# Spreading biases by TensorE, a root on ScalarE, scores that begin with high halves: one change to a fused layer kernel

## The reference

```python
xn  = (x - mean(x)) / sqrt(var(x) + 1e-5)
# branch 1, per sequence
h   = tanh(xn @ W1.T + b1)                 # 256 -> 256
s   = h @ w2.T + b2                        # one score for each token
e   = exp(s - max(s))
ctx = cumsum(e * xn) / cumsum(e)           # running mean over the tokens
a   = tanh(concat(ctx, xn) @ Wc.T + bc)    # 512 -> 256
# branch 2, integer weights / 127
f   = (silu(xn @ wg.T) * (xn @ wu.T)) @ wd.T   # 256 -> 768 -> 256
out = x + a + f
```

## Time and profile before

| | us |
|---|---|
| median of 3 runs | 412.07 |
| the profiled execution | 412.01 |
| its span, first to last instruction | 410.1 |
| TensorE busy | 391.7 |
| VectorE busy | 300.6 |
| ScalarE busy | 252.3 |
| GpSimd busy | 194.4 |

### The profile page before, as it was taken

The page is one execution under the profiler, slowest core; times in us unless marked ns, Lnnn a source line. Parts: engine busy times, 40 slices in busy tenths (PEclk is TensorE's granted clock), DMA queues, the critical chain, the costliest instruction groups (busy, mean ns, idle before and its releaser), DMA issues.

```text
span 410.1 us, 7885 instructions
## 1 busy us (share of the span) xinstructions
PE 391.7 (96%) x2742; PEld 269.3 (66%) x2742; DVE 300.6 (73%) x636; ACT 252.3 (62%) x465; POOL 194.4 (47%) x256
## 2 busy tenths in 40 slices
PE   7689989999979999899999999999999999999996
PEld 2435746675737578577768676676767677685765
DVE  3897988998896889785874857778668577755351
ACT  1797768888979775684563764536354553536250
POOL 0251342556643999868370512878707365402000
PEclk9898999999999999999999999999999999999999
DMA  6998221334334163647200012332331240101001
GB/s 207 362 349 262 54 52 40 64 57 74 74 81 127 34 131 95 136 91 143 77 28 27 26 53 55 107 98 69 90 77 40 89 105 2 51 14 41 27 26 59
DMA packets 55039, 36.84 MB, mean 90 GB/s; under 512 B 31696, under 2 KB 50384, under 8 KB 54992
## 3 DMA queue, kind: packets, MB, share of 16 engines
q1 hardware_dynamic: 54416, 35.79, 33.3%
q10 hardware_dynamic: 576, 0.46, 0.5%
HBM read 20.45 MB, written 8.45 MB: 70 GB/s over the span
## 4 chain that ended last, share of the span: by engine, by line
PE 62%; DVE 10%; POOL 8%; issue 7%; ACT 6%; DMA 4%; SPq 2%; ACTq 0%; POOLq 0%; DVEq 0%
PE bank L623 31%; PE bank L650 24%; PE bank L670 6%; POOL xt L1103 3%; POOL ex L1095 2%; DVE stats L857 2%; DMA xt<-xt 2%; SPq L1135 2%; ACT xnat L760 2%; DMA xres<-in_x 2%; POOL wide L1113 2%; DVE bank L995 2%; ACT bank L783 1%; POOL ex L1100 1%; ACT sg L789 1%
## 5 line engine op out<-in xcount | busy, mean ns | idle before, releaser
L650 PE MATMUL bank<-xt,narrow 128*128 128x512 f16 x768 | 178.2, 380 | 2.4 <-DVE sm L932 2.2
L650 PEld LDWEIGHTS bank<-xt,narrow 128*128 128x128 f16 x768 | 75.1, 98 | 79.7 <-DVE sm L932 2.7
L623 PE MATMUL bank<-narrow,xt 128*128 128x256 f16 x768 | 94.4, 276 | 5.5 <-DMA xt<-xt 2.4
L623 PE MATMUL bank<-narrow,wide 128*128 128x256 f16 x792 | 96.3, 273 | 0.0
L623 PEld LDWEIGHTS bank<-narrow,xt 128*128 128x128 f16 x768 | 75.5, 99 | 25.2 <-issue 3.5
L623 PEld LDWEIGHTS bank<-narrow,wide 128*128 128x128 f16 x792 | 77.5, 98 | 9.4
L1113 POOL TENSOR_TENSOR wide<-ex,wide 128x512 f16<-128x512 f32 x32 | 40.0, 1267 | 83.8 <-ACT wide L810 83.8
L789 ACT ACTIVATE sg<-bank 128x512 f32<-128x512 f32 x96 | 56.8, 593 | 37.2 <-PE bank L650 37.0
L995 DVE SCALAR_TENSOR_TENSOR bank<-bank,sg 128x512 f32<-128x512 f32 x96 | 65.6, 693 | 15.9 <-PE bank L650 13.5
L1000 DVE TENSOR_TENSOR wide<-bank,wide 128x512 f16<-128x512 f32 x90 | 60.4, 680 | 20.3 <-ACT wide L796 18.7
L796 ACT ACTIVATE wide<-bank 128x512 f16<-128x512 f32 x90 | 53.4, 595 | 34.2 <-DVE bank L995 33.7
(11 more groups left out here) (84 smaller groups left out, 237.4 us busy)
## 6 DMA issues: line engine op xcount, KB each, us to landing
rows<-scratch SPq DMA_DIRECT2D x16, 512.0 KB, 5.4
out_y<-xres SPq DMA_DIRECT2D x32, 256.0 KB, 2.2
xres<-in_x SPq DMA_DIRECT2D x15, 512.0 KB, 8.8
xt<-xt SPq DMA_TRANSPOSE x56, 2.5
wide<-in_wg SPq DMA_DIRECT2D x1, 768.0 KB, 9.2
wide<-in_wu SPq DMA_DIRECT2D x1, 768.0 KB, 9.8
wide<-in_wd SPq DMA_DIRECT2D x1, 768.0 KB, 11.9
xres<-in_x SPq DMA_DIRECT2D x2, 256.0 KB, 5.8
```

Source lines behind the costliest of these rows:

```text
L623: return pe.matmul(dst, lhs, rhs, start=False, stop=stop, skip_group_check=True)
L650: mm = pe.matmul(b[:, :], pg.up(which, k, j), pg.xn(sx, k, tok), start=n == 0, stop=n == len(todo) - 1)
```

## The change

- b1 with w2, and bc with b2, come as two short rows over ScalarE's DMA queue. TensorE spreads each over the partitions with a matmul by a row of ones, in bank 7; ScalarE copies the result to `every`, first b1 and w2, later bc and b2.
- The second half of block 0's x is loaded over ScalarE's queue, in front of these rows. The triangle moves to the end of SyncE's loads.
- The root of block 0: VectorE adds epsilon, ScalarE takes the square root (`Sqrt`, another function table, then Silu again), VectorE takes the reciprocal and makes one Newton step.
- Warm-up matmuls: 8, 2 and 4 around the two spreads instead of 22.
- Scores of blocks 0 and 1 start when the high halves are there and wait for low halves in front of the passes that use them. Passes now go high by high, high by low, low by high.
- The gate weights' copy to float16 (`Wgh`) goes from ScalarE to GpSimd, in front of `Wuh`.
- Planner: other durations (`V0`, `N`, `Tx`), starts, due times of checks, of blocks from 3 on (1.5 us earlier), of the statistics of block 2, and places of `M1` to `M3`.

```diff
-    "Sc": (VE, 1.85, 1.95), "V0": (VE, 0.7, 0.8), ...
-    "T": (PO, 1.35, 1.45), "N": (PO, 2.8, 2.9), ...
+    "Sc": (VE, 1.85, 1.95), "V0": (VE, 1.3, 1.4), ...
+    "T": (PO, 1.35, 1.45), "N": (PO, 2.95, 3.05), ...
-    "Lx": (SY, 0.6, 4.0), "Tx": (SY, 1.0, 4.0),
+    "Lx": (SY, 0.6, 4.0), "Tx": (SY, 2.6, 4.8),
-BEGIN = {TE: 9.1, SE: 2.5, VE: 9.9, PO: 1.0, SY: 12.0}
+BEGIN = {TE: 7.9, SE: 7.6, VE: 8.5, PO: 1.0, SY: 12.0}
-            place += [(turn + 2.6 + 0.9 * m, (f"M{m + 1}", i // BLK_SEQ, 0)) for m in range(3)]
+            place += [(turn + 2.6 + 2.0 * m, (f"M{m + 1}", i // BLK_SEQ, 0)) for m in range(3)]
+    def early(i):
+        return 0.0 if i == FIRST_T else 1.5
-            first = due["S", blocks[0], 0] - (6.5 if blocks[0] >= FIRST_T else 2.0)
+            first = due["S", blocks[0], 0] - (6.5 + early(blocks[0]) if blocks[0] >= FIRST_T else 2.0)
-                due["B", i, 0], due["B", i, 1] = first - 10.0 + 2.0 * n, first - 9.0 + 2.0 * n
+                lead = 6.0 if i == FIRST_T else 10.0
+                due["B", i, 0], due["B", i, 1] = first - lead + 2.0 * n, first - lead + 1.0 + 2.0 * n
-    for st, t in {"W1h": -3, "K1": 7, "W1l": -3, "Wgh": 2, "Wuh": -2, "Wdh": 3, "Kg": 7, "Kd": 9, "Ku": 8, "Kc": 9,
-                  "Ke": 9, "Kf": 12, ...
+    for st, t in {"W1h": -3, "K1": 7, "W1l": -3, "Wgh": -4, "Wuh": -2, "Wdh": 3, "Kg": 15, "Kd": 17, "Ku": 16, "Kc": 17,
+                  "Ke": 17, "Kf": 12, ...
-        return [(("Ss", i, x), 0), ((*turned, x), 0), *([] if i else [(("W1l", 0, 0), 0)])]
+        return [(("Ss", i, x), 0), ((*turned, x), 0.8 if turned[0] == "Xl" and not wide else 0),
+                *([] if turned[0] == "Tx" else [(("Xh", i, x), 0)]), *([] if i else [(("W1l", 0, 0), 0.4)])]
...
-                    self.passes, self.passes_int = [(0, 0), (1, 0), (0, 1)], [(0, 0), (1, 0)]
+                    self.passes, self.passes_int = [(0, 0), (0, 1), (1, 0)], [(0, 0), (1, 0)]
...
+                for sx, sw in pg.passes:
+                    if by_halves and (sx, sw) == (0, 1) and i == 0:
+                        pe.wait_ge(v_w, 1)
+                    if by_halves and sx:
+                        pe.wait_ge(*pg.x_ready(i, pr)[0])
+                    for t in range(2):
+                        tok = slice(tokens(i, pr).start + t * P, tokens(i, pr).start + (t + 1) * P)
+                        for k in range(KD):
+                            mm = onto(b[:, t * D:(t + 1) * D], pg.xn(sx, k, tok), pg.w1(sw, k), ...)
...
+            dve.wait_ge(v_mv, 2)
+            step(dve.tensor_scalar(veps[:, t], mv[:, t, 1], EPS, None, ALU.add))
+            dve.tensor_scalar(minus_half[:, t], veps[:, t], -0.5, None, ALU.mult)
+            dve.wait_ge(a_root, 1)
+            step(dve.reciprocal(rstd[:, t], rstd[:, t]))
+            ...
...
-            act.dma_start(bias[:, 0:D], biases[0:D].partition_broadcast(P)).then_inc(s_b1, 16)
-            act.dma_start(w2b2[:, :], w2b2_in.partition_broadcast(P)).then_inc(s_w2, 16)
-            act.dma_start(bias[:, D:], biases[D:2 * D].partition_broadcast(P)).then_inc(s_bc, 16)
-            act.dma_start(tri[:, :], tri_in).then_inc(s_tri, 16)
+            load_first(act, 1)
+            act.dma_start(b_row, biases.rearrange("(o d) -> o d", o=1)).then_inc(s_b, 16)
+            act.dma_start(w2_row, w2b2_in.rearrange("(o d) -> o d", o=1)).then_inc(s_w2, 16)
             act.wait_ge(v_set, 1)
-            act.activation(spare[:, SEQS:], one[:, :], ACT.Silu)
+            act.activation(spare[:, SEQS:SEQS + 1], one[:, :], ACT.Sqrt)
+            act.wait_ge(p_b, 1)
+            act.activation(every[:, 0:2 * D], bank[BANKS - 1][:, 0:2 * D], ACT.Copy).then_inc(a_b, 1)
+            act.wait_ge(v_rs0, 1)
+            act.activation(rstd[:, columns(0)], veps[:, columns(0)], ACT.Sqrt).then_inc(a_root, 1)
+            act.activation(spare[:, SEQS + 1:], one[:, :], ACT.Silu)
+            act.wait_ge(p_b, 2)
+            act.activation(every[:, 2 * D:], bank[BANKS - 1][:, 0:D + 1], ACT.Copy).then_inc(a_b, 1)
...
+            warm_up(0)
+            pe.wait_ge(v_set, 3)
+            pe.wait_ge(s_b, 16)
+            pe.wait_ge(s_w2, 16)
+            to_every(0, b_row[:, 0:D], True)
+            to_every(D, w2_row[:, 0:D], False).then_inc(p_b, 1)
+            warm_up(1)
+            pe.wait_ge(a_b, 1)
+            to_every(0, b_row[:, D:], True)
+            to_every(D, w2_row[:, D:], False).then_inc(p_b, 1)
+            warm_up(2)
             pe.wait_ge(s_ident, 16)
```

More of the change, by code:

```diff
@@ L626, in scores @@
                 b = bank_of(pg, "S", i, pr)
[L627 to L636 removed]
+                pe.wait_ge(a_ss, pg.nth("Ss", i, pr))
+                by_halves = i < FIRST_T and not pg.wide
+                if by_halves:
+                    pe.wait_ge(a_x, pg.nth("Xh", i, pr))
+                else:
+                    for s, count in pg.x_ready(i, pr):
+                        pe.wait_ge(s, count)
+                if i == 0 and not pg.wide:
+                    pe.wait_ge(a_w, 1)
+                for sx, sw in pg.passes:
[6 more added lines that the diff above has]
+                        for k in range(KD):
+                            mm = onto(b[:, t * D:(t + 1) * D], pg.xn(sx, k, tok), pg.w1(sw, k),
+                                      (sx, sw) == pg.passes[-1] and k == KD - 1)
                 mm.then_inc(p_s, 1)
@@ L899, in root_newton, with root_first, step @@
                 step(eng.tensor_tensor(rstd[:, t], rstd[:, t], newton[:, t], ALU.mult))
-            if g and NEWTON - 1 in its:
+            if NEWTON - 1 in its:
                 step(eng.tensor_tensor(shift[:, t], mv[:, t, 0], rstd[:, t], ALU.mult))
                 step(eng.tensor_scalar(shift[:, t], shift[:, t], -1.0, 0.0, ALU.mult, ALU.add))
+        def root_first(dve):
+            t, n = columns(0), [0]
+            def step(ins):
+                n[0] += 1
+                ins.then_inc(v_rs0, 1)
+                dve.wait_ge(v_rs0, n[0])
+            dve.wait_ge(v_mv, 2)
[3 more added lines that the diff above has]
+            step(dve.reciprocal(rstd[:, t], rstd[:, t]))
+            step(dve.tensor_tensor(newton[:, t], rstd[:, t], rstd[:, t], ALU.mult))
+            step(dve.tensor_tensor(newton[:, t], newton[:, t], minus_half[:, t], ALU.mult))
+            step(dve.scalar_tensor_tensor(out=rstd[:, t], in0=newton[:, t], scalar=1.5, in1=rstd[:, t],
+                                          op0=ALU.add, op1=ALU.mult))
         def root_ready(i):
@@ L1173, in halves @@
                 return w.rearrange("(k p) n -> p k n", p=P)
[L1175 to L1176 removed]
+            load_first(sp, 0)
             sp.dma_start(w1_32, halves(w1)).then_inc(s_w1, 16)
@@ L1205, in _, with warm_up, to_every @@
             pe.wait_ge(v_set, 2)
-            for n in range(WARM):
-                mm = pe.matmul(bank[n % BANKS][:, :], warm[:, 0:P], warm[:, 0:BLK], start=True, stop=True)
-            mm.then_inc(p_warm, 1)
+            last = bank[BANKS - 1]
+            def warm_up(part):
+                for n in range(WARM[part]):
+                    mm = pe.matmul(bank[n % BANKS][:, :], warm[:, 0:P], warm[:, 0:BLK], start=True, stop=True)
+                mm.then_inc(p_warm, 1)
+            def to_every(at, row, start):
+                return pe.matmul(last[:, at:at + row.shape[1]], ones[0:1, :], row, start=start, stop=True,
+                                 skip_group_check=True)
+            warm_up(0)
[9 more added lines that the diff above has]
+            warm_up(2)
             pe.wait_ge(s_ident, 16)
```

108 lines of the change are left out of this document (50 added, 58 removed).

## The result

The changed kernel takes 401.81 us (median of 4 runs, 401.60 to 403.07); the kernel before, timed beside it, 411.66 (4 runs, 410.12 to 412.25). The ratio is 0.975, 95% interval 0.971 to 0.979. The profiled execution took 401.76 us, its span is 399.9.

What follows compares the result with a forecast made beforehand. TensorE, busy 391.7 of 410.1 us, was taken as the bound, leaving only its waits and low-clock stretches to win. Terms -2.5 - 1.8 - 1.5 - 0.2 + 1.0 = -5.0 took 412.0 to 407.0 us, range 403.8 to 412.0.

Steps and rivals of the forecast that it cites:

- Part 3: Blocks 2 on: earlier due times and 2.6 us planned issue cover waits for transposed blocks; -1.5 us, bounds 0 and -2.4.
- Part 4: Softmax: steps 2.0 apart may remove the 2.19 us wait but delay the shares; -0.2 us, bounds -2.2 and +4.2.
- The delay that I feared: Softmax: the last step is placed up to 6.6 us later, and with it the shares that GpSimd waits for.
- given back at GpSimd: Rival, 131 to 176 us: later softmax delays GpSimd by 4.2, the wait before 171.03 grows; 411.4 us, chance 0.18.
- Part 1: Head: first scores at 12.75 instead of 14.66, plus 0.6 from the clock; -2.5 us, bounds -0.6 and -3.3.
- without a gap: Sign in the head: ScalarE works without a gap from 8 to 12.7 and so sets the first scores.
- that rival: Head: ScalarE stands still behind its table load (drain 1.38), or bias rows come late; 408.3 us, chance 0.05.
- Part 2: Blocks 0 and 1, 28 to 35 us: later checks and ScalarE without gate copy close the gap; -1.8, bounds 0, -3.7.
- Rest: Whole kernel: all orders are replanned, so single new waits may appear; +1.0 us, bounds 0 and +2.
- Head only: Rival: only the head gains, the other changes trade waits for others; 410.1 us (409.5 to 410.8), chance 0.12.
- The slower rival: 20 to 45 us: flag as late as 37.9, TensorE runs out of banks; 414.9 us, chance 0.13.
- four bounded gains: Head, block 0 and 1 order, blocks 2 on, softmax: -2.5, -1.8, -1.5, -0.2; near good ends, chance 0.08.

Runs made afterwards that it cites:

- e9: Changed kernel with only the planned duration of a pair of DMA transposes as in the kernel before: 407.5 us, ratio 0.988.
- e2: Changed kernel with old due times and durations for DMA-transposed blocks (no 1.5 us lead) and the old lead of block 2's statistics: 409.46 us.
- e1: Changed kernel with the softmax placed as before (TensorE's three steps 0.9 apart, V0 planned at 0.7): median 404.50 us.
- e10: Kernel before with only the planned duration of a pair of DMA transposes set to the trace's: 5.1 us faster than the kernel before (4.5 by the ratio).
- e5: Kernel before with all of the planner's new numbers, its head, root, score order and gate copy as they were: 405.69 us, ratio 0.979.
- e3: Changed kernel with the range checks due as early as before; the text gives no measured time or ratio.
- e6: Changed kernel with the gate copy back on ScalarE: ratio 0.974.
- e14: Changed kernel with the planner's old numbers, except those of moved steps, so the new head alone: 410.51 us, ratio 0.991.
- e8: Changed kernel without the 1.5 us lead of blocks 3 on: 398.59 us, ratio 0.965.
- e4: Changed kernel in which GpSimd's gate copy waits for block 0's normalised x; the text gives no measured time or ratio.
- e11: Changed kernel with the gate copy waiting for normalised x and warm-up matmuls 9, 2, 2 instead of 8, 2, 4: highest run 401.15 us.
- e15: Changed kernel without the 1.5 us lead of blocks 3 on, run again on another chip: 401.09 us, ratio 0.970.

## Why the prediction was wrong

**Part 3** is the step that failed. I read it as a cover for two waits on transposed blocks, "1.5 of the 2.4 us", and closed its bound at -2.4. The planned duration also decides whether the whole order holds: undoing it costs 5 to 6 us (e9 0.988, e2 the same with the lead undone as well), and kernels with the old duration fall 6.6 to 8.5 us behind their own plan between the flag and the second softmax, those with the true one at most 2.0. The 1.5 us lead, which I counted with it, costs about 1. What could have told me stood in the trace of before and in my own text: a pair of transposes takes 2.6 us to issue (four in 5.23 us from 130.14) and was planned at 1.0. An error of 1.5 us, for each of 28 pairs, in the plan of a queue that also carries the softmax, is not priced by the two waits where its data comes late.

**Part 4** had the wrong size and the wrong cause. The wait did go (forecast -0.2, measured -2.6 between 110 and 130), but it goes with the duration: with spaced steps and the old duration the lag still grows by 3.1 us there (e2; in e9 by 1.5, from 100 to 110 us), with close steps and the true one by 0.9 (e1) and 0.7 (e10). The delay that I feared is real: spaced steps bring the shares' store from 114.11 to 118.54 (e1, changed) and, on the old head, from 118.06 to 123.58 (e10, e5). In the profiles it costs TensorE next to nothing (the lag at 380 us is 20.0 in e1 and 20.4 in the changed kernel, 23.6 in both e10 and e5), and in the changed kernel the true duration and the earlier head outweigh it, since in the kernel before the store was at 123.58. So the rival "given back at GpSimd" had the place and the delay right and the price wrong: in the changed kernel GpSimd starts its first multiply at 125.44, before at 133.21, and where it starts at 132 (e3, e5) nothing is given back.

**Part 1**: -1.8 until 20 us where -2.5 was forecast, a fair size out of two errors. The data came earlier than I took it: second x half by 4.99 (6.7), epsilon 6.02 (7.9), rows 5.49 (6.2), gate weights on the chip at 7.5 (11.4 to 12.4). The root was ready at 7.32 (8.9). Then the gate copy on GpSimd, for which I charged nothing, met VectorE: the early weights put it beside the normalisation, and 1.29 + 1.22 us were lost. The root's result came at 9.40 (9.8), the first scores at 13.44 (12.75). ScalarE did not set them: it idles 2.18 us before it splits the transposed x at 12.74, so "without a gap" was wrong. The low level didn't lift before 15 us, so the first scores still run at the slow pace. No drain stood behind the table load: 7.33 + 1.28, and the next activation at 8.63; that rival falls. Here the trace agrees with the Trainium skill, ScalarE: Activation LUTs, section "What ACT_TABLE_LOAD costs", in the load and goes against it in the drain.

**Part 2**: the size was near, -2.4 for -1.8, with the flag at 33.80 and the level at 1.00 as named, and on the new head both causes that I gave are needed. From 20 to 35 us the lag grows by 2.5 in the changed kernel, by 4.6 with the checks early (e3), by 6.1 with the gate copy on ScalarE (e6) and by 5.9 with the new head and all old numbers (e14). In the time neither is shown to survive: with the checks early the wait before 165.90 goes, and e6's ratio can't be told from the changed kernel's. How the 2.4 split over the two was not measured. **Rest**: +1.0 was charged for new waits; there is none, the one before 171.03 shrank from 1.78 to 1.26, and the stretches outside the four lumps came out at -0.7. By stretch, the 5.3 us that the lag is off by are 1.3 in Part 3's (-2.8 for -1.5, 35 to 60 us), 2.4 in Part 4's, 1.7 in the rest and 0.6 in Part 2's, less 0.7 at the head.

"Head only" (410.1) is what e14 gives for the head by itself, 410.5 in its group, but the planner's part did not trade waits. The slower rival fell with the flag, 33.80 against 37.5 (its own sum, 35.49 + 4.2 - 1.9, is 37.8 and not 37.9). Its place was a real one: with the new numbers on the old head (e5) the flag stands at 37.0. My range was cut off at the good end: four bounded gains were all to be near their good ends at 0.08, though they hang together through one plan.

## What to carry to other kernels

Where a planner orders the work, compare its durations with the trace first, those of serial queues above all: a wrong one is a fault in every decision behind it, and its worth isn't the sum of the waits that name it. Then set a run against its plan at a few steps: where the lateness grows, the plan is wrong. Price such a change with a wide bound on the good side. When a copy moves to GpSimd, look for VectorE instructions in the same microseconds; two instructions that end together are the sign.

## What the hardware showed that I had not expected

- VectorE's normalisation of block 0 (4 instructions) took 1.38, 2.5 to 2.6 or 3.5 to 3.7 us in profiles of kernels with the same head. VectorE's timeline, the changed kernel run again and then e3:

```profile
8.25 2.58 DVE L942 TENSOR_SCALAR xnat<-xres,mv,rstd 128x256 f32<-128x256 f32 x4
```

```profile
9.16 3.50 DVE L942 TENSOR_SCALAR xnat<-xres,mv,rstd 128x256 f32<-128x256 f32 x4
```

  It depends on how many of GpSimd's two copies fall into it (none holds it up in e8, where the copy comes at 9.27, in its last part: 1.38), and so on when weights land (gate copy from 7.53 to 9.27 over these profiles). It is one source of the changed kernel's spread (399.59 to 403.85).
- The pace of TensorE in the head is another: the first 4 matmuls on rows took 1.10 to 1.29 us in some executions and 2.04 in others. In four with 2.04 (e3, e4, e9, e11) the mean granted clock over the span reads 0.999 to 1.00 although these matmuls ran at half the pace: in the head I would go by the durations of matmuls, not by the granted clock alone. Block 0's first 24 score matmuls show it most: 2.78 us in e8 and 2.83 in e15, 3.49 and 4.70 in the two profiles of the changed kernel. Of the 2.4 us of lag between e8 and the second of these, 1.9 are here.
- Broadcasts by DMA may cost more than their bytes. 300 packets fewer (q10: 576 to 276, 0.46 to 0.27 MB) and a second queue for x brought x's second half from 7.98 to 4.99 or earlier and cut the gate weights' time from issue to landing from 9.2 to 5.2 us. My estimate for the traffic alone was 1.7. The two weren't taken apart.
- What the order of passes (high halves first) is worth by itself was not tried.
